# Decoder layer: the up sums of the last stage read by ScalarE and scaled by GpSimd instead of VectorE

## The reference

```
x = x + lightning_attention(layernorm(x))       # 16 heads of 128
x = x + cross_attention(layernorm(x), ctx)      # 64 context rows, masked softmax
x = x + ffn(layernorm(x))
...
# ffn, weights and activations rounded to 8-bit floats
qx, sx, sc = quantise(x[:, up_index])           # one scale for each token, sx
g = (qx * sx) @ (qw_gate * w_scale_gate).T * sc # 1408 columns, one scale for each column
u = (qx * sx) @ (qw_up * w_scale_up).T * sc
t = silu(g) * u
qt, st, sct = quantise(t[:, down_index])
y = (qt * st) @ (qw_down * w_scale_down).T * sct
```

## Time and profile before

| | |
|---|---|
| median of 3 runs | 2697.77 us (2696.01 to 2700.08) |
| the profiled execution: its own time | 2699.37 us |
| its span, first to last instruction | 2697.60 us |
| TensorE's granted clock, mean over the span | 0.991 of full speed |
| busy: PE, DVE, ACT, POOL | 97%, 79%, 40%, 29% |

### The profile page before, as it was taken

How to read it: one execution, slowest core, us unless ns; L and a number is a source line. 1 busy time by engine, 2 the same in 40 slices (tenths; PEclk the granted TensorE clock), 3 DMA queues, 4 the chain that set the end, 5 groups by cost and what they waited for, 6 DMA issues and landing times.

```text
span 2697.6 us, 39827 instructions
## 1 busy us (share of the span) xinstructions
PE 2625.0 (97%) x14231; PEld 2173.0 (81%) x14231; DVE 2123.9 (79%) x3806; ACT 1066.4 (40%) x1786; POOL 772.8 (29%) x952
## 2 busy tenths in 40 slices
PE   6999899999999999999999999999999999999995
PEld 6888788888888888888888888888877666666662
DVE  7888977877787778778788867876657888888887
ACT  4433333433343343334344423433324445444553
POOL 3111211221131122112212211211123555555555
PEclk9999999999999999999999999999999999999998
DMA  6553322243233324343334422342265555555532
GB/s 230 180 212 141 128 104 104 102 163 121 102 136 131 122 100 137 105 147 119 126 111 147 157 94 94 118 180 94 94 227 173 148 157 161 151 147 160 162 99 54
DMA packets 182499, 366.67 MB, mean 136 GB/s; under 512 B 79264, under 2 KB 82208, under 8 KB 173600
## 3 DMA queue, kind: packets, MB, share of 16 engines
q1 hardware_dynamic: 116480, 339.74, 36.4%
q10 hardware_dynamic: 63488, 15.74, 3.2%
q0 software_dynamic: 2336, 8.65, 1.0%
HBM read 251.75 MB, written 96.61 MB: 129 GB/s over the span
## 4 chain that ended last, share of the span: by engine, by line
PE 95%; DVE 2%; issue 2%; POOL 0%; DMA 0%; ACT 0%; POOLq 0%; DVEq 0%; SPq 0%; ACTq 0%
PE bank L704 39%; PE bank L713 14%; PE bank L1356 13%; PE bank L828 9%; PE bank L788 9%; PE bank L1397 5%; PE bank L1407 2%; PE bank L1386 1%; PE bank L1377 1%; PE bank L1366 1%; PE bank L723 0%; PE bank L746 0%; DMA finish_xs<-in_pad_mask 0%; DVE finish_rt L1559 0%; DVE finish_u L1457 0%
## 5 line engine op out<-in xcount | busy, mean ns | idle before, releaser
L704 PE MATMUL bank<-attention_xT,attention_w_hi 128*128 128x512 f32 x3072 | 956.5, 392 | 2.7 <-DVE attention_xT L894 2.6
L704 PEld LDWEIGHTS bank<-attention_xT,attention_w_hi 128*128 128x128 f32 x3072 | 568.7, 189 | 114.5 <-issue 3.2
L704 PE MATMUL bank<-attention_xT,attention_w_lo 128*128 128x512 f32 x1536 | 599.6, 390 | 0.0
L531 POOL TENSOR_TENSOR attention_sq_sum<-attention_sq_sum,attention_sq 128x512 f32<-128x512 f32 x128 | 206.6, 1614 | 1228.9 <-ACT attention_sq L676 1228.9
L713 PE MATMUL bank<-attention_w_hi,attention_xT 128*128 128x256 f32 x2048 | 383.6, 288 | 3.7 <-DVE attention_sig_v L851 3.7
L704 PEld LDWEIGHTS bank<-attention_xT,attention_w_lo 128*128 128x128 f32 x1536 | 288.8, 188 | 62.1
L713 PEld LDWEIGHTS bank<-attention_w_hi,attention_xT 128*128 128x128 f32 x2048 | 321.1, 193 | 4.0 <-DVE attention_sig_v L851 4.0
L713 PE MATMUL bank<-attention_w_lo,attention_xT 128*128 128x256 f32 x1024 | 291.1, 284 | 0.0
L1356 PE MATMUL bank<-finish_w_out_hi,finish_og 128*128 128x512 f32 x824 | 284.7, 407 | 0.2
L984 DVE TENSOR_TENSOR attention_sf<-bank,attention_dcy 128x512 f32<-128x512 f32 (+1 forms) x256 | 147.8, 619 | 172.4 <-PE bank L788 172.3
L996 DVE TENSOR_TENSOR attention_sl<-attention_sf,attention_sh 128x384 fp32r<-128x384 f32 (+1 forms) x384 | 242.6, 686 | 0.0
(11 more groups left out here) (195 smaller groups left out, 4971.7 us busy)
## 6 DMA issues: line engine op xcount, KB each, us to landing
attention_xT<-normed_turned SPq DMA_DIRECT2D x62, 2048.0 KB, 8.5
gated_heads<-attention_og_out SPq DMA_DIRECT2D x64, 1024.0 KB, 7.3
finish_og<-gated_heads SPq DMA_DIRECT2D x103, 512.0 KB, 3.8
finish_og_last<-gated_heads SPq DMA_DIRECT2D x25, 512.0 KB, 3.8
normed_turned<-attention_shared SPq DMA_DIRECT2D x24, 512.0 KB, 6.6
attention_shared<-in_w_head SPq DMA_DIRECT2D x16, 512.0 KB, 7.1
finish_x<-in_x SPq DMA_DIRECT2D x32, 256.0 KB, 4.0
out<-finish_x SPq DMA_DIRECT2D x32, 256.0 KB, 4.3
```

What stands on the lines that cost most here:

```text
L531: g.tensor_tensor(sq_sum[:, col_b], sq_sum[:, col_b], sq[:, :], ALU.add).then_inc(s_acc, 1)
L704: mm = pe.matmul(dst[:, :], part[a][w][:, k, col:col + P], xT[i][:, b, k, :], start=(k == 0 and s == 0), stop=(k == KD - 1 and s == 2))
```

## The change

For each of the 96 pieces ScalarE now copies the up sums from PSUM with the token's scale into u, ahead of the silu, and GpSimd multiplies u by the column scales into t and then silu by t. VectorE makes only g. TensorE waits for both readers before it writes a pair of banks again. GpSimd counts two steps for each piece, so all waits on `s_t` are doubled. The wait for `up_sc` moves from VectorE to GpSimd. `gate_up_scale` waits until ScalarE has read the scale that it overwrites.

```
     def gpsimd(g):
         def silu_up(m, i):
             k, (a, w) = m * NF + i, FS[i]
+            g.wait_ge(s_u, k + 1)
+            if k == 0:
+                g.wait_ge(s_up, 1)
+            after(g, s_ts, m)
+            g.tensor_tensor(t_[:, a:a + w], u_[k % 2][:, 0:w], up_sc[:, a:a + w], ALU.mult).then_inc(s_t, 1)
+            g.wait_ge(s_t, 2 * k + 1)
             g.wait_ge(s_gs, k + 1)
-            g.wait_ge(s_u, k + 1)
-            after(g, s_ts, m)
-            g.tensor_tensor(t_[:, a:a + w], sg[k % 2][:, 0:w], u_[k % 2][:, 0:w], ALU.mult).then_inc(s_t, 1)
+            g.tensor_tensor(t_[:, a:a + w], sg[k % 2][:, 0:w], t_[:, a:a + w], ALU.mult).then_inc(s_t, 1)
...
         def silu(m, i):
             k, (a, w) = m * NF + i, FS[i]
+            act.wait_ge(s_gu, 2 * k + 2)
+            act.wait_ge(s_sx, m + 1)
+            after(act, s_t, 2 * k - 2)
+            nc.scalar.activation(u_[k % 2][:, 0:w], GU[k % 2][1][:, 0:w], ACT.Copy, scale=sx[:, m % 2:m % 2 + 1]
+                                 ).then_inc(s_u, 1)
             act.wait_ge(s_g, k + 1)
-            after(act, s_t, k - 1)
             nc.scalar.activation(sg[k % 2][:, 0:w], g_[k % 2][:, 0:w], ACT.Silu).then_inc(s_gs, 1)
...
+            after(pe, s_g, k - 1)
             after(pe, s_u, k - 1)
...
-                v.wait_ge(s_up, 1)
-            after(v, s_t, k - 1)
+            after(v, s_t, 2 * k - 2)
             v.scalar_tensor_tensor(out=g_[k % 2][:, 0:w], in0=GU[k % 2][0][:, 0:w], scalar=sx[:, m % 2:m % 2 + 1],
                                    in1=gate_sc[:, a:a + w], op0=ALU.mult, op1=ALU.mult).then_inc(s_g, 1)
-            v.scalar_tensor_tensor(out=u_[k % 2][:, 0:w], in0=GU[k % 2][1][:, 0:w], scalar=sx[:, m % 2:m % 2 + 1],
-                                   in1=up_sc[:, a:a + w], op0=ALU.mult, op1=ALU.mult).then_inc(s_u, 1)
...
         def gate_up_scale(m):
             v.wait_ge(s_rs3, m + 1)
+            after(v, s_u, NF * (m - 1))
...
         def t_scale(m):
-            v.wait_ge(s_t, NF * m + NF)
+            v.wait_ge(s_t, 2 * (NF * m + NF))
```

## The result

The changed kernel takes 2706.32 us (median of 9 runs, 2704.95 to 2708.87), the kernel before on the same chip 2697.77 us (9 runs, 2693.97 to 2700.08). The interval lies above 1.002, so this is more than the 0.2% that a measurement here can tell from nothing. It spans 5.9 to 11.6 us, so it can't tell 7.9 from 8.6; only the timelines show how near the forecast came. The profiled execution took 2706.65 us, with a span of 2704.9.

A forecast was written before the change was run, and what follows sets the result against it. TensorE bounds the steady tiles, the loop through t the end, where GpSimd and VectorE exclude each other. Tiles 28 to 31 add 0.1 + 1.0 + 3.2 + 3.55 = 7.9 us to 2697.77: 2705.7, range 2699 to 2711.

The forecast's parts named there:

- Two regimes, steady tiles cost 0: TensorE sets the steady tiles, the loop through t the end; VectorE's saved 1.85 us a tile becomes waits: cost 0.
- The copy: ScalarE's added copy of the up sums from PSUM: 0.67 us, or 0.57 for 384 columns, with no new table load.
- Tile 28, +0.1; tile 29, +1.0: First two end tiles: t_scale at 2638.2 against 2638.13, as GpSimd uses up VectorE's gain; then 2654.6 against 2653.57.
- Tiles 30 and 31, turn of 15.1: +3.2 and +3.55: Last two turns, t_scale to t_scale: 15.1 us each against 11.86 and 11.54, costing 3.2 and 3.55 us.
- the 8.36: Late turn after t_round_sum: six GpSimd products and t_round_out one behind the other, and 0.03 to t_scale: 8.36 us.
- The last stretch can't change: Last t_scale to the end: 20.63 us with no gate or up piece left, so the change can't touch its length.
- My upper bound: GpSimd keeps the ports between products, 1.6 us more a turn, +3.2; TensorE's lower clock adds 1 to 2: 2711.
- Rival (a), the extra product hides: End: a column product runs in GpSimd's idle time, so no change; 2699.6, up to +5.4 us; chance 0.18.
- Rival (b), VectorE bounds the end: End: each of the four last tiles saves VectorE's 1.85 us, faster at 2690.4; chance 0.07.
- Rival (c), steady tiles slip: ScalarE or GpSimd run late and TensorE stalls in 28 tiles: 0.5 us each, 14 us, 2720; chance 0.09.
- Rival (d), VectorE loses the hand-over: Shared port pair at the end: the waiting VectorE instruction loses each hand-over; 2708.9, inside the forecast's range, no own chance.

The follow-up runs named there:

- early copy: Changed kernel with the column product written into u and, for tiles 29 to 31, piece 0's copy ahead of t_magnitude and t_scaled: 2704.98 us, ratio 1.0031.
- the same with one product: Changed kernel with the column product left out and, for tiles 29 to 31, piece 0's copy ahead of t_magnitude and t_scaled: 2697.01 us, ratio 0.9996.
- TensorE kept busy: Changed kernel plus unused matmuls, 18 and 32 of 512 columns, ahead of the last two down: 2704.81 us, ratio 1.0027.

## Why the prediction was right, point by point

- **Two regimes, steady tiles cost 0.** Right: 616.98 against 616.99 us, and 28 changed tiles alone give a ratio of 1.0009. VectorE's busy time came out at 384 and not 372. The 1.85 us a tile did go, and x_round_out, which now waits for a product that ends sooner, took 1.15 instead of 1.45 us; but centred (L1497), which now meets a column product, takes 1.47 where it took 0.78, 24 x 0.68 = 16 us. I had walked the period for TensorE's slack and not for who meets whom at centred. It costs nothing, as VectorE's waits for TensorE hide it.
- **The copy.** 0.684 and 0.561 us measured for 0.67 and 0.57 estimated between 0.59 and 0.71. At the end it lies on the path in tile 29's turn at most, where 0.01 is not to be seen. The Trainium skill's figures ("ScalarE: Activation LUTs", section "What ACT_TABLE_LOAD costs"), by which I had named 0.71 as an estimate, are 3 to 4% above the measurement; the trace decides. No table load joined it.
- **Tile 28, +0.1; tile 29, +1.0.** -0.05 and +0.90. The reason given for tile 28, that GpSimd uses up all that VectorE gained, is borne out by the kernel without the column product: there the same 1.6 us show.
- **Tiles 30 and 31, turn of 15.1: +3.2 and +3.55.** 15.08 and 15.44; in the kernel with only the end changed 15.08 and 15.09, with only the last tile changed 15.07. The order at each hand-over and the pieces of the 8.36 are those of the forecast. The 0.35 too much in the changed kernel's last turn lies ahead of them: t_round_sum started 2673.44 - 2672.98 = 0.46 us after t_scaled had ended, where the kernel before had 0.11 there. It doesn't look like chance: the three kernels made from the changed one (early copy, the same with one product, TensorE kept busy) have the 0.46 too, and those with only the end or the last tile changed or without the column product have 0.11. What sets it is open. One thing goes with it: in exactly the four executions with 0.46 an 8 KB packet of instructions (queue q14) starts 0.7 to 1.0 us behind the start of t_round_sum, and in the other six none starts within 1.5 us of it. No run shows that the one makes the other.
- **The last stretch can't change.** This step failed in the profile, by 0.84, though this doesn't follow the change: I had read "no piece left in it" as a fixed length, while it holds two `down` whose 11 matmuls take 2.55 to 4.88 us by the granted clock. My upper bound had 1 to 2 us for that.
- **How much of the hit is luck.** The four turns came to 7.97 us where 7.85 were forecast, and that isn't luck in the main, as their pieces agree; but in it 0.35 us too much in the last turn stand against 0.25 too little at tiles 28 and 29. That the median is within 0.7 us of the forecast is partly luck: the last stretch had another 0.84 in the profiled execution, the start of `finish` moves by more than that, and the interval is 5.7 us wide.
- **Rival (a), the extra product hides.** It fell: 8.55, not 1.8. Its reason was right but half of it: besides the copy's place in ScalarE's queue, t was a second lock, since the product into t must wait for the scaling of the tile before. With both taken away one product of a turn hides, 2.5 us of 8.8.
- **Rival (b), VectorE bounds the end.** With GpSimd's second product gone and the copy early the stage is 2.2 us shorter, not 7.4: 1.6 at tile 28 and under 0.5 in each later turn. So VectorE sets the pace of tile 28 and hardly that of the others, where the row of products and rounding does.
- **Rival (c), steady tiles slip.** Nothing of it: 500 of 500 us, no wait of TensorE for u or g from 2100 to 2600 us.
- **Rival (d), VectorE loses the hand-over.** It fell by the rows of the last turn: t_round_out, waiting since 2678.20, went when the ports came free at 2678.76, ahead of the product that GpSimd issued at 2678.85. That product came a little late, so the harder case is one of before, where the next product had been issued 0.05 us ahead of the hand-over and still came second. The Trainium skill's "SBUF — State Buffer", section "SBUF: two separate sides", says who starts first keeps the pair, and the trace agrees in every such pair above; in both cases it went to the one that had waited.

## What to carry to other kernels

Ask of each regime of a stage by itself what a moved instruction costs: here 28 of 32 tiles took 3.7 us more of GpSimd and 1.9 of copies on ScalarE each for nothing, and the four without cover paid 8 us. An instruction of VectorE that reads PSUM was not in the way of GpSimd (the last gate piece at 2677.67 ran for 0.62 us inside a product that took its usual 1.27), so trading it for a GpSimd product puts work into the one row that both share; count that row, product by product, where both engines meet. Before a copy is moved to another engine, look at what stands ahead of it in that engine's queue and at who waits for the bank that it frees: with the second product gone, the copy put TensorE 1.5 us back in a turn, and together with slower matmuls that made the turn 1.4 us longer.

## What the hardware showed that I had not expected

- At a hand-over between GpSimd's products and VectorE's instructions of two SBUF tensors the waiting instruction went first in every row read. In the `finish` stages of all ten profiles no such VectorE instruction saw two products end while it waited. A blocked one then takes 1.47 or 1.48 us (1408 columns, 1.62 unblocked) on VectorE and 1.12 to 1.14 on GpSimd (512 columns, 1.27 unblocked).
- The same 11 matmuls took 4.06, 4.88 or 2.55 us at a granted clock of 0.62, 0.50 and 1.00. Which of the first two it was did not follow the length of the wait ahead: 4.36 and 7.61 us went with 4.06, 4.49 and 7.31 with 4.87 and 4.88.
- The last turning DMA took 3.57 to 3.60 us from issue to use in nine of ten profiles and 5.22 in the tenth, the only one in which a 16 KB packet of instructions ran among its packets. That the packet was the cause isn't tested.
- An untouched stage of 2000 us ended anywhere within 6 us in ten profiles, which is more than most edits to the stage behind it are worth.
